# A graph network on one core: a squared tanh moved to ScalarE, a gate that reads PSUM, 23 of 50 row tiles weighed ahead, two gradient products moved up

## The chip, the cores and the metric

The kernel runs on one core of one Trainium2 chip. The metric is the device time of one execution in microseconds (us). TensorE (PE) multiplies matrices into PSUM, its accumulation memory of 8 banks of 512 fp32 columns; VectorE (DVE), ScalarE (ACT) and GpSimd (POOL) do the rest; SyncE (SP) only issues DMA transfers. Each engine runs its own instructions in the order in which they are written, and the engines meet only at semaphores (`wait_ge`, `then_inc`). An instruction that waits holds up all that stand behind it on its engine.

## The reference

x is 6250 nodes by 32 features; there are 106,250 directed edges (src, dst), sorted by dst. Four residual blocks follow one another: attention over the edges, five layers of graph convolution with normalisation, a gradient block, and a mean over the neighbours. The change touches the third, where the derivative of a scalar with respect to x is wanted:

```
def get_H(xx):
    z = xx @ W_fc.T
    e = sigmoid(concat([z[src], z[dst]]) @ W_attn.T)
    w = exp(e - emax[dst])
    h = segment_sum(w / denom[dst] * z[src], dst)
    h1 = segment_sum((h @ W_encK.T + b_encK)[src], dst)
    K = mlp3(h1, K_w0, K_b0, K_w1, K_b1, K_w2, K_b2)
    ue = (h @ W_p1.T + b_p1)[src] + (h @ W_p2.T + b_p2)[dst]
    U = mlp3(ue, ...)      # per edge: w2 @ relu(w1 @ tanh(w0 @ ue + b0) + b1) + b2
    return sum(segment_sum(K[src] * U, dst))
dHdx = grad(get_H)(x)      # then dHdx @ J.T - dHdx @ D.T
```

Its backward pass needs, for every edge, the tanh t of the first layer of U, its slope 1 - t*t, and the gate "relu of the second layer is above zero"; for every pair of nodes that has edges, the weight exp(sigmoid) and its derivative; and for every node three products that add up to the gradient of h.

## The kernel before

Edges lie as 128 partitions by 832 columns. Node data lies as 50 row tiles of 128 nodes (`NT` = 50). Sums over edges that can't be done by a scan over sorted edges are done as dense products with a table of counts, 6400 by 6400, that lies in DRAM.

The parts that matter here follow one another in this order:

- **The edge network ("the MLP loop"), 26 steps of 32 edge columns each.** A step's tanh values are `UT` (128 x 2048). They are taken in four pieces (`UG` = 4): PE transposes a piece (L2381) to `psT`, ACT copies it to SBUF (L2212), PE adds bias (L2395) and weight product (L2400) into one of **two** PSUM banks `psO`, ACT writes the relu to `UM` (L2214). DVE makes the slope as -t*t (L1963, 128 x 2048), the gate `hb` times the K row of the edge (L1967, four pieces), and PE and ACT take `hb` down through the transposed weights (L2381, L2235, L2417); DVE multiplies by the slope (L1977), copies (L1982) and runs a scan over sorted edges (L624, L629). Ahead of each step stands another scan (`spread_step`, L624 and L629) that repeats a node's row over its edges, and the sum that is fed to tanh (L1955). In DVE's order the gates of step k stand first, then `spread_step(k + 1)`, then the multiplication by the slope and the scan of step k. In ACT's order `up_act(k + 1)` (tanh, copies and relus) is followed by the store of step k, by `source_act(k + 2)` (L2197, which turns the loaded rows round into `UXP`), and that by `mask_act(k + 2)` (L2201, L2203), for which `spread_step(k + 2)` on DVE waits.
- **GpSimd beside it** gathers rows for the loop: 52 groups of 16 indirect DMAs (L485, `arena<-t_a`), and after these scatters the loop's results to `xd`: again 52 groups of 16 (L488), each with a load of its rows (L2525). After scatter group `HD_AT` = 29 it runs `ends_pool("umlp")`: one fetch to `joined`, a wait for DVE's `ends_dve`, a put, and 50 fetches of the loop's sums. After group `GK_AT` = 37 it fetches the rows that the K side needs.
- **Weighing ahead.** After the MLP loop, ACT and DVE make the weights of every third row tile (`BEFORE`, 17 of 50), for both halves of the columns and as two pieces each: 4 x 17 = 68 pieces of 128 x 1600 (tanh L1098, exp L1101, square L1103 on ACT; L1115 and L1120 on DVE). A piece's two results are stored to `weighed_cells` (1.6 MB). DVE does `ends_dve("umlp")` only behind all of them.
- **The K side and four quarters of a dense product** (L801, L747, L787, L869), while GpSimd goes on scattering.
- **The last scan ("dsum"),** 26 steps, once all is scattered, then `ends_pool("dsum")`.
- **The gradient of h,** `to_nodes_pe("dhf", ...)` (L787, L790): for each of 50 tiles three products (`DFM1` with `WD1`, `DFM2` with `WD2`, `SUMS3` with `fold`) into one place in PSUM. Only `DFM2` comes from the last scan.
- **The back stage:** two phases of 50 row tiles. A tile that was weighed ahead is read from DRAM (two pieces of 1.6 MB) into a ring of five buffers; the others are made by ACT (L1028, L1030, L1032) and DVE (L1042, L1048) as two pieces each. PE takes either (L1053).

The order is written out by hand on every engine; no planner chooses it.

Of the kernel before, what the change touches and what calls it, by code (L numbers as in the profile page):

```python
# [8 lines left out]
P = 128  # L9
# [69 lines left out]
def build(nc, x_in, src_in, dst_in, src_t_in, w_in, weights_in, vectors_in, out):  # L79
    ctx = ExitStack()  # L80
    with ctx:
# [146 lines left out]
        BEFORE = range(0, NT, 3)  # L228
# [143 lines left out]
        ALIAS_AT, XK_AT, GK_AT, HD_AT = 768, 15, 37, 29  # L372
# [421 lines left out]

        def to_features_pe(pe, name, source, banks):
# [295 lines left out]
        def ahead_act(act):  # L1091
            act.wait_ge(S["crossed"], TURN["umlp"] + 1)
            base = 4 * NS
            for i, j, phase, t, h in ahead():
                if j % len(BEFORE) == 0 and h == 0:
                    act.wait_ge(S[f"other{phase}"], 16 * 2)
                tanh = AHEAD_TANH[i % 2]
                act.activation(tanh, piece_of(AHEAD_OTHER[phase], h), ACT.Tanh, bias=a_dst[:, t:t + 1])  # L1098
                act.drain()
                act.wait_ge(S["weighed"], base + max(0, 2 * i - 1))  # L1100
                act.activation(AHEAD_EXP, tanh, ACT.Exp, scale=0.5, bias=half[:]).then_inc(S["weights_made"], 1)  # L1101
                act.wait_ge(S["weighed"], base + 2 * i)
                act.activation(AHEAD_SQUARE, tanh, ACT.Square).then_inc(S["weights_made"], 1)  # L1103
# [508 lines left out]
        def _(dve):  # L1612
# [346 lines left out]
            for k in range(2 * IT):  # L1959
                b = k % 2  # L1960
                slope, hb, dr = rows(UG2[b], 64), rows(UHB, 64), rows(UDR[b], 64)
                dve.wait_ge(S["umlp_tanh"], UG * (k + 1))
                dve.scalar_tensor_tensor(slope, rows(UT, 64), -1.0, rows(UT, 64), ALU.mult, ALU.mult)  # L1963
                for u in range(UG):
                    t = slice(8 * u, 8 * u + 8)
                    dve.wait_ge(S["umlp_relu"], UG * k + u + 1)
                    dve.scalar_tensor_tensor(hb[:, t, :], turned(UM[b], 64)[:, t, :], 0.0, turned(UXP[b], 64)[:, t, :], ALU.is_gt,  # L1967
                                             ALU.mult).then_inc(S["umlp_slope"], 1)
# [3 lines left out]
                for u in range(UG):  # L1972
# [4 lines left out]
                    last = dve.scalar_tensor_tensor(dr[:, t, :], slope[:, t, :], 1.0, DTURN[u % 2].rearrange("p (j f) -> p j f", f=64),  # L1977
# [82 lines left out]
            for made, t, got in node_banks("dhf", 32, bank):  # L2060
# [90 lines left out]
        def _(act):  # L2151
# [53 lines left out]
            def up_act(k):  # L2205
# [4 lines left out]
                for u in range(UG):  # L2210
# [4 lines left out]
                                   psO[u % 2].rearrange("p (j f) -> p j f", f=64), ACT.Relu).then_inc(S["umlp_relu"], 1)  # L2215

# [12 lines left out]
            for k in range(2 * IT):  # L2229
# [3 lines left out]
                for u in range(UG):  # L2233
                    act.wait_ge(S["umlp_turned"], 2 * UG * k + UG + u + 1)
                    act.copy(packB[u % 2], psT[u % 2]).then_inc(S["umlp_turned_copied"], 1)  # L2235
# [51 lines left out]
        def _(pe):  # L2287
# [96 lines left out]
            def up_pe(k):  # L2384
                n = 2 * UG * k
                for u in range(UG + 1):
# [350 lines left out]
```

## Time and profile before

| | us |
|---|---|
| median of 3 runs | 9476.88 (9472.27 to 9494.99) |
| the profiled execution | 9485.84 |
| its span | 9484.0 |

| engine | busy us | share |
|---|---|---|
| PE | 4877.8 | 51% |
| DVE | 4601.9 | 49% |
| ACT | 2819.5 | 30% |
| POOL | 5429.2 | 57% |

No engine is busy all the time, since the parts have different limits. One has to read each part by itself: where it starts and ends, which engine works without a gap in it, and for what the others wait. The profiled execution's own time is 1.8 us above its span.

### The profile page before, as it was taken

Reading aid. Unit: us, or ns where it says so; the run is one execution under the profiler, and the core shown is the slowest. Engines: PE = TensorE matmul, PEld = TensorE weight load, DVE = VectorE, ACT = ScalarE, POOL = GpSimd, SP = SyncE. Lnnn points to the kernel's source line nnn. Section 1 sums busy time; section 2 is a strip of 40 time slices with the busy share of each in tenths; the row PEclk is TensorE's granted clock in tenths of the full one; section 3 lists DMA queues with packets and bytes.
Section 4 is the critical chain, followed back from the end, with each engine's and each line's share of the span. In section 5 each row is a group of like instructions: output and inputs, shape, how many; then the busy total and the mean of one; then the engine's idle time right before and its main releaser. Section 6 shows DMA issues by size and latency. Waiting matters only on the chain.

```text
span 9484.0 us, 77287 instructions
## 1 busy us (share of the span) xinstructions
PE 4877.8 (51%) x27914; PEld 2625.5 (28%) x27914; DVE 4601.9 (49%) x6100; ACT 2819.5 (30%) x2192; POOL 5429.2 (57%) x5420
## 2 busy tenths in 40 slices
PE   1000007999257777775577665344440035038976
PEld 0000006888112232331222222244430023032333
DVE  5677776777000000000298960388885510428870
ACT  0111110000000000000198950266667600429850
POOL 3777767777777777777520017688877777320000
PEclk5555555555578989887698975676765568559986
DMA  8666536443398989999799999455559948538767
GB/s 186 215 222 220 205 83 137 154 153 141 155 415 356 415 359 411 365 362 415 279 283 268 288 204 379 144 202 206 203 191 370 342 147 336 187 85 282 263 222 291
DMA packets 1203136, 2404.24 MB, mean 254 GB/s; under 512 B 566439, under 2 KB 818794, under 8 KB 1171354
## 3 DMA queue, kind: packets, MB, share of 16 engines
q1 hardware_dynamic: 996986, 2076.35, 61.7%
q0 software_dynamic: 187136, 170.29, 6.9%
q10 hardware_dynamic: 18720, 153.79, 4.2%
q8 instruction: 171, 2.80, 0.1%
q14 instruction: 123, 1.01, 0.0%
HBM read 1606.44 MB, written 711.62 MB: 244 GB/s over the span
## 4 chain that ended last, share of the span: by engine, by line
POOL 37%; DMA 25%; issue 12%; PE 11%; ACT 7%; ACTq 4%; DVE 3%; SPq 1%; DVEq 0%; POOLq 0%
POOL arena L485 18%; DMA arena<-cells_w 14%; POOL xd L488 9%; POOL cells_w L488 9%; DMA arena<-cells_c 8%; PE ps L698 6%; ACT arena L1030 3%; ACTq L1029 3%; ACT arena L1028 2%; PE ps L787 2%; PE ps L879 1%; ACTq L2266 1%; PE ps L1053 1%; PE ps L1161 1%; DMA arena<-hot 1%
## 5 line engine op out<-in xcount | busy, mean ns | idle before, releaser
L698 PE MATMUL ps<-arena 128*64 128x458 f32 (+2 forms) x7252 | 1349.0, 655 | 701.2 <-DMA arena<-cells_w 699.7
L485 POOL DMA_INDIRECT arena<-t_a,arena x832 | 945.9, 1137 | 1094.9 <-DMA t_a<-arena 841.7
L1053 PE MATMUL ps<-arena 128*33 128x400 f32 x6336 | 1165.1, 522 | 310.1 <-DVE arena L1048 302.4
L488 POOL DMA_INDIRECT sorted<-arena x832 | 839.7, 1009 | 288.9 <-issue 288.9
L716 DVE COPY carry<-ps 64x128 f32<-64x128 f32 (+1 forms) x5 | 1.5, 295 | 2048.2 <-PE ps L698 2048.2
L488 POOL DMA_INDIRECT xd<-arena x832 | 832.7, 1001 | 256.4 <-issue 253.2
L488 POOL DMA_INDIRECT cells_c<-arena x832 | 810.5, 974 | 292.6 <-issue 292.6
L488 POOL DMA_INDIRECT cells_w<-arena x832 | 813.0, 977 | 276.8 <-issue 276.8
L485 POOL DMA_INDIRECT arena<-t_kv,idx x832 | 816.9, 982 | 258.7 <-issue 253.3
L698 PEld LDWEIGHTS ps<-arena 128*64 128x64 f32 (+1 forms) x7252 | 426.2, 147 | 1621.1 <-issue 856.4
L1053 PEld LDWEIGHTS ps<-arena 128*33 128x33 f32 x6336 | 366.6, 115 | 1106.4 <-issue 652.8
L1555 ACT ACTIVATE norm_cols<-norm_cols 128x1 f32<-128x1 f32 x5 | 1.0, 203 | 2235.0 <-DVE norm_cols L1537 2235.0
L1042 DVE TENSOR_TENSOR arena<-arena 128x1600 f32<-128x1600 f32 x328 | 597.3, 1821 | 96.0 <-ACT arena L1032 42.9
L1270 PE MATMUL ps<-arena 128*128 128x50 bf16 x832 | 72.4, 219 | 1055.3 <-DVE arena L1258 1055.3
L1048 DVE SCALAR_TENSOR_TENSOR arena<-arena 128x1600 f32<-128x1600 f32 x328 | 598.8, 1826 | 25.9
L629 DVE TENSOR_TENSOR_SCAN arena<-ps,arena 128x512 f32<-128x512 f32 (+2 forms) x494 | 591.4, 1263 | 7.6
L1030 ACT ACTIVATE arena<-arena,half 128x1600 f32<-128x1600 f32 x328 | 534.5, 1630 | 24.5 <-issue 2.4
L1369 PE MATMUL ps<-arena,packT 128*128 128x50 f32 x1664 | 434.8, 412 | 0.0
L1369 PEld LDWEIGHTS ps<-arena,packT 128*128 128x128 f32 x1664 | 434.7, 336 | 0.0
L879 PE MATMUL ps<-arena 128*64 128x400 f16 x1568 | 280.9, 508 | 248.3 <-DMA arena<-cells_c 227.6
L1032 ACT ACTIVATE arena<-arena 128x1600 f32<-128x1600 f32 x246 | 374.2, 1521 | 0.0
L801 PE MATMUL ps<-ident,arena 128*64 128x128 f32 x300 | 20.7, 308 | 652.4 <-DVEq L209 651.7
(536 smaller groups left out, 9097.3 us busy)
## 6 DMA issues: line engine op xcount, KB each, us to landing
arena<-cells_w SPq DMA_DIRECT2D x245, 3200.0 KB
arena<-cells_c SPq DMA_DIRECT2D x294, 800.0 KB, 5.3
arena<-cells_turned SPq DMA_DIRECT2D x200, 800.0 KB, 8.5
cells_w<-arena SPq DMA_DIRECT2D x49, 3200.0 KB, 20.4
weighed_cells<-arena SPq DMA_DIRECT2D x68, 1600.0 KB, 14.4
arena<-weighed_cells SPq DMA_DIRECT2D x68, 1600.0 KB, 7.2
cells_c<-arena SPq DMA_DIRECT2D x50, 1600.0 KB, 5.8
cells_turned<-arena SPq DMA_DIRECT2D x100, 800.0 KB, 5.4
```

Of the source, the lines that this page charges most:

```text
L485: return pool.indirect_dma_start(dst, None, table, bass.IndirectOffsetOnAxis(ap=index, axis=0))
L488: return pool.indirect_dma_start(table, bass.IndirectOffsetOnAxis(ap=index, axis=0), source, None)
L629: dve.tensor_tensor_scan(to[:, piece], mask[:, 0:n * CJ], buf[:, piece], 0.0, ALU.mult, ALU.add)
L698: mm = pe.matmul(bank[base + k][g * f:(g + 1) * f, 0:m], rows_of, tile[:, g * width + at:g * width + at + m], start=first, stop=last, skip ...
L879: mm = pe.matmul(bank[(4 if i == 0 else 0) + c][64 * g:64 * g + 64, 0:400], pieces, moving[:, a:a + 400], start=first, stop=last, skip_gro ...
L1029: act.drain()
L1030: last = act.activation(expo[b], tanh[b], ACT.Exp, scale=0.5, bias=half[:])
L1032: last = act.activation(tanh[b], tanh[b], ACT.Square)
L1042: last = dve.tensor_tensor(expo[b], expo[b], piece_of(counts_of(name, p), h), ALU.mult)
L1048: dve.scalar_tensor_tensor(tanh[b], tanh[b], -1.0, expo[b], ALU.add, ALU.mult).then_inc(S["weighed"], 1)
L1053: last = pe.matmul(bank[4 * h + c][64 * kind:64 * kind + 33, 0:400], own[:, t, :], moving[:, 400 * c:400 * c + 400], start=t == 0, stop=do ...
L1369: pe.matmul(to[:, 0:NT], packT[k % 2][:, i * P:(i + 1) * P], snap[k % 2][:, i * NT:(i + 1) * NT], start=True, stop=True, skip_group_check= ...
```

## The change

Four edits, in the places named above.

1. **MLP loop.** DVE's slope instruction (L1963) goes. ACT squares `UT` into `UG2` behind the four relus of a step. The sign is put into the copy of the transposed gates (scale -1) and into the constant of L1977. The gates `hb` read `psO`, the PSUM bank, where they read `UM`. So PE may write a bank of `psO` only once DVE has read it: a second wait stands before L2395.
2. **Weighing ahead.** 23 of 50 row tiles, spread evenly, where there were 17: 92 pieces and not 68. ACT's tanh of the next piece is issued between the exp and the square of this one.
3. **Places in GpSimd's row.** `HD_AT` 29 becomes 33, `GK_AT` 37 becomes 41.
4. **Gradient of h.** The products of `DFM1` and of `SUMS3` are made before PE's part of the last scan's end, into banks 4 to 7; only the product of `DFM2` is left behind it.

```diff
-        BEFORE = range(0, NT, 3)
+        BEFORE = [t for t in range(NT) if t * 23 % NT < 23]
...
-        ALIAS_AT, XK_AT, GK_AT, HD_AT = 768, 15, 37, 29
+        ALIAS_AT, XK_AT, GK_AT, HD_AT = 768, 15, 41, 33
...
+        def gradient_pe(pe, source, weight, first):
+
+            if not first:
+                pe.wait_ge(S["fm_taken"], STEP["dhf"])
+            for t in range(NT):
+                to = bank[4 + t // 16][:, t % 16 * 32:t % 16 * 32 + 32]
+                g, at = t // (NT // 2), t % (NT // 2) * P
+                a = slice(64 * g, 64 * g + 64)
...
+                last = pe.matmul(to, source[a, at:at + P], weight[a, :], start=first and t % 16 == 0, stop=not first,
+                                 skip_group_check=True)
+                if first:
+                    last = pe.matmul(to, SUMS3[0:96, t * P:t * P + P], fold[32][0:96, 0:32], start=False, stop=False,
+                                     skip_group_check=True)
...
             for k in range(2 * IT):
                 b = k % 2
                 slope, hb, dr = rows(UG2[b], 64), rows(UHB, 64), rows(UDR[b], 64)
-                dve.wait_ge(S["umlp_tanh"], UG * (k + 1))
-                dve.scalar_tensor_tensor(slope, rows(UT, 64), -1.0, rows(UT, 64), ALU.mult, ALU.mult)
                 for u in range(UG):
                     t = slice(8 * u, 8 * u + 8)
                     dve.wait_ge(S["umlp_relu"], UG * k + u + 1)
-                    dve.scalar_tensor_tensor(hb[:, t, :], turned(UM[b], 64)[:, t, :], 0.0, turned(UXP[b], 64)[:, t, :], ALU.is_gt,
-                                             ALU.mult).then_inc(S["umlp_slope"], 1)
+                    dve.scalar_tensor_tensor(hb[:, t, :], psO[u % 2].rearrange("p (j f) -> p j f", f=64), 0.0,
+                                             turned(UXP[b], 64)[:, t, :], ALU.is_gt, ALU.mult).then_inc(S["umlp_slope"], 1)
...
                                    psO[u % 2].rearrange("p (j f) -> p j f", f=64), ACT.Relu).then_inc(S["umlp_relu"], 1)
+                act.activation(UG2[k % 2], UT, ACT.Square)
...
                     if UG * k + v >= 2:
                         pe.wait_ge(S["umlp_relu"], UG * k + v - 1)
+                        pe.wait_ge(S["umlp_slope"], UG * k + v - 1)
...
+            await_made(pe, "dh_made")
+            gradient_pe(pe, DFM1, WD1, True)
             ends_pe(pe, "dsum", OD, 64, bank[3])
             await_made(pe, "dd_made")
             to_features_pe(pe, "DD", nodes(DD, 64), 4)
-            await_made(pe, "dh_made")
-            to_nodes_pe(pe, "dhf", DFM1, 64, 32, lambda c: WD1[64 * c:64 * c + 64, :], bank,
-                        more=((DFM2, 64, lambda c: WD2[64 * c:64 * c + 64, :]), (SUMS3, 96, lambda c: fold[32][0:96, 0:32])))
+            gradient_pe(pe, DFM2, WD2, False)
```

On PE, in the third and fourth product of a step's way up; before (L2381 is the transposition, L2395 the bias, L2400 the weight product):

```order
L2381 MATMUL ps<-ident,arena 128x128 [waits umlp_turned_copied,umlp_tanh]
L2381 MATMUL ps<-ident,arena 128x128 x3
L2395 MATMUL ps<-bias_parts,ones_bf 128x512 [waits umlp_relu]
L2400 MATMUL ps<-weights,packT 128x128 [waits umlp_turned_copied]
L2400 MATMUL ps<-weights,packT 128x128 x3
L2395 MATMUL ps<-bias_parts,ones_bf 128x512 [waits umlp_relu]
```

and now (L2407, L2422, L2427 are the same three):

```order
L2407 MATMUL ps<-ident,arena 128x128 [waits umlp_turned_copied,umlp_tanh]
L2407 MATMUL ps<-ident,arena 128x128 x3
L2422 MATMUL ps<-bias_parts,ones_bf 128x512 [waits umlp_slope,umlp_relu]
L2427 MATMUL ps<-weights,packT 128x128 [waits umlp_turned_copied]
L2427 MATMUL ps<-weights,packT 128x128 x3
L2422 MATMUL ps<-bias_parts,ones_bf 128x512 [waits umlp_slope,umlp_relu]
```

The order is the same; the bias product now waits for `umlp_slope`, which DVE's gates give. For the third product of step k it is the first gate of step k.

On ACT, the end of one step's way up and what stands behind it; before (L2214 relu, L2241 store, L2197 `source_act`, L2201 and L2203 `mask_act`):

```order
L2212 COPY packT<-ps 128x512
L2214 ACTIVATE arena<-ps 128x8x64
L2241 DMA d_edges<-arena 128x2048
L2197 COPY arena<-arena 128x4096
L2201 CAST ps<-same_s 128x16x31
L2203 CAST first_same<-same_s 128x1
```

and now, with what each waits for (L2241 is now the square, L2267 the store, L2222 `source_act`):

```order
L2237 COPY packT<-ps 128x512 [waits umlp_turned]
L2239 ACTIVATE arena<-ps 128x8x64 [waits umlp_up]
L2241 ACTIVATE arena<-arena 128x2048
L2267 DMA d_edges<-arena 128x2048 [waits umlp_taken]
L2222 COPY arena<-arena 128x4096 [waits umlp_slope,loaded1]
L2226 CAST ps<-same_s 128x16x31 [waits scanned]
L2228 CAST first_same<-same_s 128x1
```

One instruction is added, between the last relu and the store.

On PE, from the end of the quarters to the back stage, now (L889 quarters, L807 and L810 `gradient_pe`, L664 the end of the last scan, L821 the transposition of its sums; L807 below it is the product of `DFM2`):

```order
L889 MATMUL ps<-arena 96x400 x3
L807 MATMUL ps<-folded,arena 128x32 [waits made]
L810 MATMUL ps<-fold,arena 128x32
...
L664 MATMUL ps<-carry,equal_d 128x64 [waits carried]
L821 MATMUL ps<-ident,arena 64x128 [waits fm_taken,made]
...
L807 MATMUL ps<-folded,arena 128x32 [waits fm_taken]
L807 MATMUL ps<-folded,arena 128x32 x24
L807 MATMUL ps<-folded,arena 128x32 [waits group_done]
L807 MATMUL ps<-folded,arena 128x32 x24
```

100 of the 150 products stand ahead of L664 now; before, all stood behind it, three to a tile.

## Rows read from the trace of the kernel before

**Rows 1.** The page's part 4, the chain that ended last, by engine

```profile
POOL 37%; DMA 25%; issue 12%; PE 11%; ACT 7%; ACTq 4%; DVE 3%; SPq 1%; DVEq 0%; POOLq 0%
```

**Rows 2.** Timeline, one step: start us, us, engine, line, what, [idle before <-releaser]

```profile
6528.51 7.42 ACT L2197 COPY arena<-arena 128x4096 f32<-128x4096 f32 x1 [0.49 <-DMA arena<-a_edges]
6529.03 2.29 DVE L1963 SCALAR_TENSOR_TENSOR arena<-arena 128x2048 f32<-128x2048 f32 x1
...
6536.56 0.47 DVE L624 SCALAR_TENSOR_TENSOR arena<-spread_carry,first_same,arena 128x128 f32<-128x128 f32 x1 [0.85 <-ACT first_same L2203]
...
6555.64 0.38 PE L2395 MATMUL ps<-bias_parts,ones_bf 128*128 128x512 bf16 x1
...
6556.04 1.16 PE L2400 MATMUL ps<-weights,packT 128*128 128x128 f32 x8
...
6557.23 1.03 ACT L2214 ACTIVATE arena<-ps 128x512 f32<-128x512 f32 x1 [1.25 <-PE ps L2400]
...
6558.08 0.62 ACT L2212 COPY packT<-ps 128x512 f32<-128x512 f32 x1
```

**Rows 3.** Single lines: count, ns min/median/max, first and last start us

```profile
L1963 DVE SCALAR_TENSOR_TENSOR arena<-arena x26: 2291/2293/2297, 6092.4 to 7079.6; 128x2048 f32<-128x2048 f32 x26
...
L1967 DVE SCALAR_TENSOR_TENSOR arena<-arena x104: 1086/1177/1342, 6095.7 to 7085.0; 128x512 f32<-128x512 f32 x104
...
L1977 DVE SCALAR_TENSOR_TENSOR arena<-arena,ps x104: 664/687/715, 6118.7 to 7090.9; 128x512 f32<-128x512 f32 x104
...
L1032 ACT ACTIVATE arena<-arena x246: 1517/1521/1527, 4707.3 to 9139.8; 128x1600 f32<-128x1600 f32 x123
```

**Rows 4.** Timeline: from the MLP loop's end to the last piece weighed ahead

```profile
7119.33 0.80 PE L664 MATMUL ps<-carry,equal_s 128*128 128x128 f32 x2 [28.50 <-DVEq L649]
7127.37 1.63 ACT L1098 ACTIVATE arena<-arena,a_dst 128x1600 f32<-128x1600 f32 x1 [14.78 <-DMA arena<-row_a_src]
...
7552.20 1.82 DVE L1120 SCALAR_TENSOR_TENSOR arena<-ps,arena 128x1600 f32<-128x1600 f32 x1
```

**Rows 5.** Stage 7127 to 7553: span, busy of PE, PEld, DVE, ACT, POOL, PEclk, DMA, GB/s

```profile
7127.00:7553.00 426.00, 0.00 (x0) 0.00 (x0) 247.06 (x136) 315.02 (x204) 326.95 (x346) 0.50 1.05 373
```

**Rows 6.** DMA queues from 7140 to 7540: packets, MB, share of 16 engines

```profile
q1 hardware_dynamic: 82453, 129.51, 90.8%
q0 software_dynamic: 12458, 19.98, 14.2%
```

**Rows 7.** Timeline of GpSimd and DVE: two group loads, the join

```profile
7116.83 0.58 POOL L2525 DMA_DIRECT2D arena<-d_edges  x1
...
7137.81 0.58 POOL L2525 DMA_DIRECT2D arena<-d_edges  x1
...
7631.13 1.00 POOL L485 DMA_INDIRECT joined<-runs,join_s  x1 [0.30 <-issue]
...
7633.78 0.29 DVE L655 TENSOR_TENSOR joined<-joined,ps 128x128 f32<-128x128 f32 x1 [79.75 <-DMA joined<-runs,join_s]
```

**Rows 8.** Timeline of GpSimd: three gather instructions of one MLP step

```profile
6530.07 2.07 POOL L485 DMA_INDIRECT arena<-t_a,arena  x1 [0.30 <-issue]
...
6532.44 4.09 POOL L485 DMA_INDIRECT arena<-t_a,arena  x1 [0.30 <-issue]
...
6550.68 0.94 POOL L485 DMA_INDIRECT arena<-t_a,arena  x1 [0.30 <-issue]
```

**Rows 9.** Timeline of DVE: the start of the last scan

```profile
8175.72 1.03 DVE L2039 COPY arena<-arena 128x1024 f32<-128x1024 f32 x1 [113.69 <-DMA arena<-xd]
```

**Rows 10.** Timeline of PE: the three gradient products, two tiles

```profile
8449.16 0.63 PE L787 MATMUL ps<-folded,arena 64*128 64x32 f32 x2
...
8450.71 0.63 PE L787 MATMUL ps<-folded,arena 64*128 64x32 f32 x2
```

**Rows 11.** Timeline of PE in the back stage; a row is three tiles

```profile
8711.26 16.31 PE L1053 MATMUL ps<-arena 128*33 128x400 f32 x96 [0.83 <-DVE arena L1048]
8728.42 16.31 PE L1053 MATMUL ps<-arena 128*33 128x400 f32 x96 [0.84 <-DVE arena L1048]
```

More of the change, by code:

```diff
@@ L793, in to_nodes_pe @@
                     last.then_inc(S["fm_made"], 1)
+        def gradient_pe(pe, source, weight, first):
[5 more added lines that the diff above has]
+                a = slice(64 * g, 64 * g + 64)
+                if t == NT // 2:
+                    last.then_inc(S["group_done"], 1)
+                    groups_done[0] += 1
+                    pe.wait_ge(S["group_done"], groups_done[0])
+                last = pe.matmul(to, source[a, at:at + P], weight[a, :], start=first and t % 16 == 0, stop=not first,
[3 more added lines that the diff above has]
+                                     skip_group_check=True)
+                elif t % 16 == 15 or t == NT - 1:
+                    last.then_inc(S["fm_made"], 1)
         def to_features_pe(pe, name, source, banks):
@@ L1093, in ahead_act, with tanh_act @@
             base = 4 * NS
-            for i, j, phase, t, h in ahead():
+            todo = list(ahead())
+            def tanh_act(i):
+                _, j, phase, t, h = todo[i]
                 if j % len(BEFORE) == 0 and h == 0:
                     act.wait_ge(S[f"other{phase}"], 16 * 2)
-                tanh = AHEAD_TANH[i % 2]
-                act.activation(tanh, piece_of(AHEAD_OTHER[phase], h), ACT.Tanh, bias=a_dst[:, t:t + 1])
+                act.activation(AHEAD_TANH[i % 2], piece_of(AHEAD_OTHER[phase], h), ACT.Tanh, bias=a_dst[:, t:t + 1])
+            tanh_act(0)
+            for i in range(len(todo)):
                 act.drain()
                 act.wait_ge(S["weighed"], base + max(0, 2 * i - 1))
-                act.activation(AHEAD_EXP, tanh, ACT.Exp, scale=0.5, bias=half[:]).then_inc(S["weights_made"], 1)
+                act.activation(AHEAD_EXP, AHEAD_TANH[i % 2], ACT.Exp, scale=0.5, bias=half[:]).then_inc(S["weights_made"], 1)
+                if i + 1 < len(todo):
+                    tanh_act(i + 1)
                 act.wait_ge(S["weighed"], base + 2 * i)
-                act.activation(AHEAD_SQUARE, tanh, ACT.Square).then_inc(S["weights_made"], 1)
+                act.activation(AHEAD_SQUARE, AHEAD_TANH[i % 2], ACT.Square).then_inc(S["weights_made"], 1)
         def ahead_dve(dve):
@@ L1976, in _ @@
                         dve.wait_ge(S[f"d_kept{b}"], CREDIT + 16 * (k // 2))
-                    last = dve.scalar_tensor_tensor(dr[:, t, :], slope[:, t, :], 1.0, DTURN[u % 2].rearrange("p (j f) -> p j f", f=64),
+                    last = dve.scalar_tensor_tensor(dr[:, t, :], slope[:, t, :], -1.0, DTURN[u % 2].rearrange("p (j f) -> p j f", f=64),
                                                     ALU.add, ALU.mult)
@@ L2059, in _ @@
             dhf = nodes(DHF, 32)
-            for made, t, got in node_banks("dhf", 32, bank):
+            for made, t, got in node_banks("dhf", 32, bank[4:8]):
                 dve.wait_ge(S["fm_made"], made)
@@ L2234, in _ @@
                     act.wait_ge(S["umlp_turned"], 2 * UG * k + UG + u + 1)
-                    act.copy(packB[u % 2], psT[u % 2]).then_inc(S["umlp_turned_copied"], 1)
+                    act.activation(packB[u % 2], psT[u % 2], ACT.Copy, scale=-1.0).then_inc(S["umlp_turned_copied"], 1)
                 if k >= 1:
```

## The prediction

> **What bounds the kernel now.** I read the chain of waits first: by engine, 37% of it is GpSimd, 25% DMA and 11% PE [rows 1]. Followed in order of time, it runs on GpSimd from the middle of the MLP loop until all results are scattered, then over the last scan, then over PE in the back stage. So an edit counts only as far as it moves GpSimd's row of gathers and scatters, the last scan, or PE behind it.
>
> Then the timeline of one step of the MLP loop [rows 2]. DVE starts the slope at 6529.03 and the next `spread_step` at 6536.56, 7.53 us later, having waited 0.85 us for ACT's mask. ACT began to turn the next rows round (L2197) at 6528.51, before DVE's gates. That is what makes the loop fit: ACT's relus of a step are done while DVE is still in its scan. A step takes (7079.6 - 6092.4) / 25 = 39.5 us by the starts of L1963 [rows 3].
>
> Then the hand-over. The loop ends at about 7120, weighing ahead runs from 7127.4 to 7554.0 [rows 4], and DVE has then idled 79.75 us when GpSimd comes to the join at 7631.1 [rows 7]. So the join waits for GpSimd now, and DVE is 80 us early. A scatter group takes 7137.81 - 7116.83 = 20.98 us [rows 7]. The last scan starts at 8175.7, where DVE has waited 113.69 us for scattered rows [rows 9]: the K side and the quarters are hidden with that much to spare. In the back stage PE works 16.31 us of every 17.16 [rows 11].
>
> **The MLP loop.** The new wait says: the third product of step k may start only once DVE has done the first gate of step k. On DVE this gate stands behind the whole scan of step k - 1. On ACT, the relus of pieces 3 and 4 stand ahead of the square, the next source copy and the next mask, and for this mask DVE waits with its next `spread_step`. So what ran beside the scan is now a chain behind it, once a step:
> - first gate: between 0.69 (L1977, one operand in PSUM) and 1.18 (L1967, both in SBUF) [rows 3]; I take 0.93;
> - bias and product 0.38 + 1.16, relu 1.03, copy 0.62, product 1.16, relu 1.03 [rows 2]: 5.4, and with some 0.05 for each of six hand-overs 5.7;
> - the square of 128 x 2048: at least the 1.52 of 1600 columns (L1032), at most the 2.29 that DVE needs for the same size [rows 3]; by columns 1.52 x 2048 / 1600 = 1.95; I take 1.9;
> - from the start of the source copy to the start of `spread_step`, 6536.56 - 6528.51 = 8.05 [rows 2].
>
> Together 16.6 us from DVE's first gate to its next `spread_step`, against 7.53: 9.1 a step. The removed 2.29 of DVE and the shorter gates are inside this and buy nothing, as DVE waits for ACT. I take 9.0 (8 to 10). For 25 steps this is 225 us, and about 3 for the last, in which the square stands ahead of the first copy downward: the loop ends 228 us later, and the first piece is weighed at 7355 and not at 7127.
>
> **Weighing ahead.** A piece takes (7554.0 - 7127.4) / 68 = 6.27 us [rows 4]. ACT is busy for 315.02 / 68 = 4.63 of it, and the DMA engines are full, at a share of 1.05 and 373 GB/s [rows 5]; so the reordered tanh buys nothing here. 14.2 points of the share are GpSimd's own scatters [rows 6]. Once GpSimd stands still, a piece can take 6.27 x 90.8 / 105 = 5.4; I take 5.5 (4.63 to 6.27).
>
> When does GpSimd stand still? It comes to the join 4 groups later, 4 x 20.98 = 84, but earlier by what DVE no longer costs it: beside L1963 and L1967 its gathers take 2.07 and 4.09 us where 0.94 is the rule, and beside L1977 0.94 [rows 8, 2], so 1.13 + 3.15 = 4.3 a step and up to 111 in 26. That makes 7631 + 84 - 111 = 7604 (up to 7715). From 7355 to 7604 there are 249 / 6.27 = 39.6 pieces, and the other 52.4 take 288: 7892, and with the last stores in flight (a piece and a half) 7900. GpSimd waits there some 300 us, and all 18 scatter groups left are queued behind that wait, as are the fetches for the K side.
>
> The join is thus at 7900 where it was at 7634 [rows 7]: +266. Behind it stand 18 groups and not 22: -84. The last scan starts 182 us later, at about 8358. The K side and the quarters move by 266 as well, since `GK_AT` keeps its distance of 8 groups from `HD_AT`; of the 113.69 us to spare [rows 9] some 30 are left, so they cost nothing.
>
> **The gradient products.** A tile's three products take 8450.71 - 8449.16 = 1.55 us [rows 10], so one takes 0.52 (at most its 0.63 of busy time). Behind the last scan 50 tiles now take 26 us and not 78: -51 (-46 to -52). The other 100 products, 52 us, lie between 8175.7 and 8449 of before [rows 9, 10], where PE has nothing but the ends of the scan to do.
>
> **The back stage.** A row of 96 is six pieces: 2.72 us of PE each, 272 for the 100 of a phase, and a wait of 0.84 in every three tiles, 14 us a phase [rows 11]. With 54 made pieces and not 66, ACT and DVE are ahead, and up to 28 us in both phases could go. But a phase now reads 46 x 1.64 + 27 x 0.82 = 97.5 MB, 261 us at the 373 GB/s of [rows 5], beside PE's 272: nearly two bounds at once. I take half, -14 (-28 to +5).
>
> **Sum.** +182 - 51 - 14 = +117 on the profiled execution's 9485.8: 9603. The median of the runs is 9 lower: 9594. The bounds: 8 to 10 us a step is 25 either way in the loop and, since fewer pieces then lie beside GpSimd's scatters, 22 in the sum; a piece at 4.63 or 6.27 is -46 or +40; GpSimd at 7715 is +14; then +5 and -14 to +19. The forecast's own range is 9520 to 9670.
>
> **Rivals.**
> - *The loop keeps its pace.* The gate in PSUM costs nothing, and the freed DVE and GpSimd time comes through. For it: PE and ACT both have gaps in a step (1.25 us before each relu [rows 2]). Against it: the gate is behind the scan in DVE's own order, and no gap of PE can change that. Then weighing ahead starts at 7127, 76 pieces are done by 7604, the other 16 by 7692, the join is at 7700: +66 - 84 - 51 - 14 = -83, median 9394. It decides if a step stays under about 42 us. If GpSimd's stalls also stay as they are, it comes at 7715, the join moves by 84, and -65 is left: 9412.
> - Where that rests on GpSimd: the rows show gathers of 4.09 us beside an instruction with two inputs in SBUF and 0.94 beside one with a PSUM input [rows 8]. The Trainium skill (SBUF — State Buffer, "Who interferes with whom") says that a VectorE instruction with at most one SBUF input does not contend with GpSimd, and the trace agrees. It also says that one with two contends only with GpSimd instructions that read SBUF, and infers that making DMA descriptors needs the write side alone; by that there would be nothing to free, and the rival's time would be 9412. The 4.09 speaks against that part.
> - *The loop loses half of it,* 4.5 us a step, as ACT finds the third product sooner than I think, or a later load sets the pace either way. Then 113 us of the delay go, 101 in the sum: +16, median 9493, no change that can be told. Against it: the terms of the chain are all from rows, and only the square and the first gate are estimates, 1.3 us between them.
> - *The back stage turns DMA-bound.* At 330 GB/s its 97.5 MB take 295 us a phase where a phase takes 286 now (50 / 3 x 17.16): +9 a phase and not -7, median 9626, inside the forecast's range.
>
> **How the numbers follow.** The forecast, with the DMA-bound back stage in it, has 0.80; the loop at its old pace 0.13; half 0.07. Under 0.3%, 28 us, this kernel's change can't be told from none: so faster means under 9448, and that is the first rival alone, 0.13; no change is most of the third, 0.06; slower is the rest, 0.81. The range of 9480 to 9680 takes in nearly all of the forecast and part of the third; the first rival stays out.
>
> **What would show it.** In the profile after: starts of the gates 48.5 us apart, where L1963 had 39.5; DVE idle for some 9 us before L624 of `spread_step`, released by ACT's mask; PE's bias product released by DVE; the loop's end near 7348. Weighing ahead near 5.5 us a piece once GpSimd is still. GpSimd idle for about 300 us before its put of `joined`, released by DVE. Gathers of 4 us gone. The last scan starting near 8358, DVE idle there about 30 us. 26 us from the first `DFM2` product to the last. PE in the back stage with gaps under 0.8 us in three tiles, released by DMA if at all. The forecast is wrong if the gates come 40 us apart, if GpSimd doesn't wait at the join, or if weighing ahead is not held by DMA.

## The result, and the profile after

| | before | after |
|---|---|---|
| median | 9483.46 us (4 runs, 9472.27 to 9494.99) | 9565.3 us (4 runs, 9558.28 to 9572.54) |
| profiled execution | 9485.84 | 9572.54 |
| its span | 9484.0 | 9570.7 |

The changed kernel takes 1.0086 times as long [1.0074, 1.0098]. Predicted was 9594, with a range of 9480 to 9680.

The chain of waits of the kernel after, by engine, to be read against [rows 1]: GpSimd has lost 14 points of the span; DVE, DMA and PE have gained 8, 5 and 5. Up to the join the end is now reached over the MLP loop (DVE's scans, PE, ACT) and weighing ahead, not over GpSimd's gathers and scatters; behind the join it still runs over GpSimd's scatters.

```profile
DMA 30%; POOL 23%; PE 16%; DVE 11%; issue 9%; ACT 7%; ACTq 3%; DVEq 1%; SPq 1%; POOLq 0%
```

The timeline of one step of the MLP loop after, all engines, in order of start. The last column is the idle time before it and what ended it. It answers to [rows 2, 8].

```profile
6522.12 1.06 POOL L485 DMA_INDIRECT arena<-t_a,arena  x1 [0.30 <-issue]
6522.45 1.94 DVE L1992 SCALAR_TENSOR_TENSOR arena<-ps,arena 128x512 f32<-128x512 f32 x2
6523.49 0.95 POOL L485 DMA_INDIRECT arena<-t_a,arena  x1 [0.30 <-issue]
6523.60 0.59 PE L2422 MATMUL ps<-bias_parts,ones_bf 128*128 128x512 bf16 x1 [8.53 <-DVE arena L1992]
...
6525.93 1.03 ACT L2239 ACTIVATE arena<-ps 128x512 f32<-128x512 f32 x1 [9.80 <-PE ps L2427]
...
6529.49 1.90 ACT L2241 ACTIVATE arena<-arena 128x2048 f32<-128x2048 f32 x1
...
6531.28 7.11 ACT L2222 COPY arena<-arena 128x4096 f32<-128x4096 f32 x1
...
6539.02 0.53 DVE L624 SCALAR_TENSOR_TENSOR arena<-spread_carry,first_same,arena 128x128 f32<-128x128 f32 x1 [8.27 <-ACT first_same L2228]
```

Read it as a chain. DVE's first gate (L1992) starts at 6522.45. PE has waited 8.53 us for it with the bias of the third piece (L2422); ACT has waited 9.80 us for PE. Two relus with a copy of a transposed piece between them, the square (1.90) and the source copy (7.11) follow, and only then the mask, for which DVE has waited 8.27 us (0.85 before). From first gate to next `spread_step` it is 6539.02 - 6522.45 = 16.57 us; the prediction's sum was 16.6.

The gates as one line, (count, ns min/median/max, first and last start), and then `spread_step`'s first instruction from the groups by line of 6080 to 7320 us (count, busy us, mean ns, idle before):

```profile
L1992 DVE SCALAR_TENSOR_TENSOR arena<-ps,arena x104: 1002/1030/1054, 6095.9 to 7294.3; 128x512 f32<-128x512 f32 x104
```

```profile
L624 DVE SCALAR_TENSOR_TENSOR arena<-spread_carry,first_same,arena 128x128 f32<-128x128 f32 x25 | 11.8, 474 | 199.7 <-ACT first_same L2228 199.7
```

DVE's wait for the mask is 199.7 / 25 = 8.0 us a step. The gates of one step and the next start 6570.33 - 6522.45 = 47.9 us apart. Over all 25 intervals the mean is (7287.03 - 6095.88) / 25 = 47.65: 8.2 above the 39.5 of [rows 3].

Then the hand-over: ACT's last copy of the loop (released by DVE's last carry, L631, at 7313.96), its first piece weighed ahead, GpSimd's fetch for the join, DVE's last piece, the join, GpSimd's put behind it, and DVE at the start of the last scan. They answer to [rows 4, 7, 9].

```profile
7314.32 7.14 ACT L2247 COPY arena<-arena 128x4096 f32<-128x4096 f32 x1 [7.05 <-DVE carry L631]
...
7337.11 1.63 ACT L1120 ACTIVATE arena<-arena,a_dst 128x1600 f32<-128x1600 f32 x1 [15.66 <-DMA arena<-row_a_src]
...
7604.64 1.00 POOL L485 DMA_INDIRECT joined<-runs,join_s  x1 [0.30 <-issue]
...
7869.04 1.82 DVE L1147 SCALAR_TENSOR_TENSOR arena<-ps,arena 128x1600 f32<-128x1600 f32 x1
7880.98 0.29 DVE L655 TENSOR_TENSOR joined<-joined,ps 128x128 f32<-128x128 f32 x1 [10.12 <-DMA weighed_cells<-arena]
...
7881.57 0.98 POOL L488 DMA_INDIRECT runs<-joined,join_s x1 [275.93 <-DVEq L656]
...
8338.77 1.04 DVE L2064 COPY arena<-arena 128x1024 f32<-128x1024 f32 x1 [30.45 <-DMA arena<-xd]
```

The idle time has changed sides. Before, DVE stood 79.75 us at the join and GpSimd arrived last; now GpSimd stands 275.93 us, and DVE arrives last. The stretch of weighing ahead, cut where GpSimd stops (span, then busy of PE, PEld, DVE, ACT, POOL, then PEclk, DMA share, GB/s; [rows 5]):

```profile
7337.00:7604.00 267.00, 0.00 (x0) 0.00 (x0) 154.15 (x85) 196.77 (x130) 205.07 (x217) 0.50 1.05 374
7604.00:7875.00 271.00, 0.00 (x0) 0.00 (x0) 181.30 (x100) 220.93 (x146) 1.34 (x2) 0.50 1.06 379
```

The DMA share is full in both. What GpSimd's scatters leave goes to ACT and DVE, whose busy shares rise by 11% and 16%.

PE at the gradient and at the start of the back stage; a row is one group of products ([rows 10]):

```profile
8597.72 7.76 PE L821 MATMUL ps<-ident,arena 128*64 128x128 f32 x100 [69.98 <-DVEq L209]
8606.26 19.46 PE L807 MATMUL ps<-folded,arena 64*128 64x32 f32 x100 [0.78 <-DVE arena L2083]
8631.95 7.64 PE L1073 MATMUL ps<-arena 128*33 128x400 f32 x32 [6.23 <-DVEq L209]
```

And inside the back stage, PE after ([rows 11]), with a window of 240 us that starts 74 us behind the stage's first product, after and then before:

```profile
8739.81 67.38 PE L1073 MATMUL ps<-arena 128*33 128x400 f32 x400 [1.50 <-DVE arena L1068]
...
8811.32 70.06 PE L1073 MATMUL ps<-arena 128*33 128x400 f32 x416 [0.77 <-DVE arena L1068]
```

```profile
8706.00:8946.00 240.00, 233.35 (x1388) 82.62 (x1384) 186.81 (x113) 199.49 (x129) 0.00 (x0) 0.99 0.99 353
```

```profile
8600.00:8840.00 240.00, 226.39 (x1334) 77.04 (x1332) 223.77 (x126) 235.36 (x154) 0.00 (x0) 1.00 0.82 288
```

PE's rows are longer (400 products without a wait, where 96 were) and the gaps fewer: in the whole stage PE waits for DVE 12 times and 36.1 us, where it was 31 times and 52.2, and one wait near the start is 24.5 us of either. So, that one apart, 11.6 us are left to gain there by more tiles, and DMA's share has gone from 0.82 to 0.99.

The 86.7 us between the two spans, by stretch:

| stretch | before | after | difference |
|---|---|---|---|
| start of the last scan | 8175.7 | 8338.8 | +163.1 |
| the last scan | 259.0 | 258.9 | -0.1 |
| its end to the back stage's first product | 90.8 | 34.2 | -56.6 |
| two phases of the back stage | 690.8 | 668.4 | -22.4 |
| what follows | 267.7 | 270.4 | +2.7 |

### The profile page after: what moved, and what is told of

The parts are those of the page before. It is cut to its first block, busy times and chain, and to the rows that moved or that the text cites. A ratio compares the mean times of both kernels' runs of the same rounds, so it can differ in the third digit from the quotient of the medians.

```text
span 9570.7 us, 77448 instructions
## 1 busy us (share of the span) xinstructions
PE 4858.6 (51%) x27914; PEld 2632.1 (28%) x27914; DVE 4529.2 (47%) x6068; ACT 2859.7 (30%) x2224; POOL 5329.3 (56%) x5420
## 4 chain that ended last, share of the span: by engine, by line
DMA 30%; POOL 23%; PE 16%; DVE 11%; issue 9%; ACT 7%; ACTq 3%; DVEq 1%; SPq 1%; POOLq 0%
DMA arena<-cells_w 14%; POOL arena L485 10%; POOL cells_w L488 9%; DMA arena<-cells_c 8%; PE ps L698 5%; DVE arena L629 4%; PE ps L1073 4%; DMA weighed_cells<-arena 4%; POOL xd L488 3%; ACT arena L2222 2%; ACT arena L1050 2%; ACTq L1049 1%; PE ps L787 1%; ACT arena L1048 1%; PE ps L2444 1%
## 5 line engine op out<-in xcount | busy, mean ns | idle before, releaser
L485 POOL DMA_INDIRECT arena<-t_a,arena x832 | 832.4, 1001 | 1095.3 <-DMA t_a<-arena 842.0
L1062 DVE TENSOR_TENSOR arena<-arena 128x1600 f32<-128x1600 f32 x304 | 553.5, 1821 | 172.4 <-DMA arena<-cells_turned 127.1
L1068 DVE SCALAR_TENSOR_TENSOR arena<-arena 128x1600 f32<-128x1600 f32 x304 | 555.0, 1826 | 24.3 <-issue 0.4
L1050 ACT ACTIVATE arena<-arena,half 128x1600 f32<-128x1600 f32 x304 | 495.4, 1629 | 21.8 <-issue 1.0
L2444 PE MATMUL ps<-weights,arena 128*128 128x128 f32 x832 | 192.5, 416 | 471.9 <-ACT arena L2261 247.1
L821 PE MATMUL ps<-ident,arena 128*64 128x128 f32 x300 | 21.2, 312 | 689.4 <-DVEq L209 688.7
```

Of the source, the lines that this page charges most:

```text
L485: return pool.indirect_dma_start(dst, None, table, bass.IndirectOffsetOnAxis(ap=index, axis=0))
L1050: last = act.activation(expo[b], tanh[b], ACT.Exp, scale=0.5, bias=half[:])
L1062: last = dve.tensor_tensor(expo[b], expo[b], piece_of(counts_of(name, p), h), ALU.mult)
L1068: dve.scalar_tensor_tensor(tanh[b], tanh[b], -1.0, expo[b], ALU.add, ALU.mult).then_inc(S["weighed"], 1)
L2444: last = pe.matmul(DTURN[v % 2][:, i * P:(i + 1) * P], packB[v % 2][:, i * P:(i + 1) * P], weights[:, down:down + P], start=True, stop=True)
```

## The experiments

Theory: PE's wait for the first gate makes the step 8 us longer; everything ahead of the last scan follows from it; ScalarE's square, the 23 tiles and the gradient save a little each. Rivals: the square itself, or the read of PSUM, costs the time; or the six extra tiles do. ACT's reordered tanh in weighing ahead stays in all runs but b.

**Undo the loop's edit alone (a_noloop).** The first of each pair is the kernel after; ACT's copies downward and the constant of the multiplication by the slope get their old signs as well:

```
-  dve.scalar_tensor_tensor(hb[:, t, :], psO[u % 2]..., 0.0, turned(UXP[b], 64)[:, t, :], ALU.is_gt, ALU.mult)
+  dve.wait_ge(S["umlp_tanh"], UG * (k + 1))
+  dve.scalar_tensor_tensor(slope, rows(UT, 64), -1.0, rows(UT, 64), ALU.mult, ALU.mult)
+  dve.scalar_tensor_tensor(hb[:, t, :], turned(UM[b], 64)..., 0.0, turned(UXP[b], 64)[:, t, :], ALU.is_gt, ALU.mult)
-  act.activation(UG2[k % 2], UT, ACT.Square)
-  pe.wait_ge(S["umlp_slope"], UG * k + v - 1)
```

> The changed kernel with the MLP loop as it was before (slope on DVE, gates from UM, no second wait on PE, copies with scale 1); 23 tiles, HD_AT 33, GK_AT 41 and the split gradient stay. The theory (the gate's wait makes the loop longer, and GpSimd then stands at the join): the loop ends at 7120 again, 92 pieces at 6.27 us end at 7704, and with the last stores 12 us later DVE is at the join at 7716, where GpSimd comes at 7631 + 84 = 7715. Join +84, 18 groups behind it and not 22: -84. Gradient -57 and back stage -22 as measured in the changed kernel: span 9408, ratio to before 0.992. The rival that weighing 24 more pieces is what costs: still slower than before, ratio above 1.003.

Measured: 9421.51 us, ratio 0.9931 [0.9915, 0.9948]. The slope starts 39.7 us apart, the join is at 7716.73, and DVE idles 32.33 us ahead of the last scan. So all the other edits together make the kernel faster, and the loop's edit alone turns this round.

**The loop's edit alone on the kernel before (b_looponly).** The same lines the other way.

> The kernel before with the MLP loop of the changed one, nothing else. The theory: a step takes 47.7 us as in the changed kernel, the loop ends some 210 us later, at 7329; GpSimd comes to the join at 7520 and stands there until 68 pieces are done: 29 beside its scatters, 39 at 5.3 us, 7739 with the last stores. So +105 us: ratio 1.011. The rival that the loop is hidden behind GpSimd (it was early at the join before): ratio within 0.3% of 1.

Measured: 9590.01, ratio 1.0105 [1.0088, 1.0122]. The join is at 7741.0, and DVE's idle time before the last scan stays at 112.7: nothing else has taken the delay up. GpSimd is at the join 110 us earlier (7521.3, before 7631.1) and waits there for it. The loop's edit costs 101 us here (1.05%) and 144 in the kernel after (9565.3 - 9421.5); f, below, shows where most of the difference lies.

```profile
7741.63 0.97 POOL L488 DMA_INDIRECT runs<-joined,join_s x1 [219.34 <-DVEq L656]
```

**The loop's edit in two halves (c_squareonly, d_gateonly).** The first is the kernel after with gates from `UM` and without PE's wait; the second keeps these two and lets DVE make the slope.

> The changed kernel, but the gates read UM in SBUF as before and PE doesn't wait for them; ACT still squares. The theory that the wait is the cause: the square lies behind relus that are done beside the scan, and the source copy starts 1.3 us later than the load alone would let it; a step takes 40.0 to 40.8 us, the loop ends 15 to 35 us later than before, the span is 9410 to 9440, ratio 0.992 to 0.996. The rival that ScalarE is the bound and its square the cause: a step near 47 us, ratio near 1.009.

> The changed kernel, but DVE makes the slope as before (L1963, 2.2 us ahead of the gates) and ACT doesn't square; the gates read PSUM and PE waits for them. The theory: the chain loses the square's 1.9 us and gains the slope's 2.2 ahead of it: a step takes 48 us, ratio 1.008 to 1.012. The rival that the square is the cause: a step near 39.5 us and a ratio near 0.992.

Measured: c 9417.3, ratio 0.9928 [0.9911, 0.9945]; d 9599.79, ratio 1.0114 [1.0097, 1.0131]. The slope of d has its starts 48.65 us apart, those of a 39.7; the gates of c about 39.9:

```profile
L1990 DVE SCALAR_TENSOR_TENSOR arena<-arena x26: 2291/2292/2294, 6095.8 to 7312.1; 128x2048 f32<-128x2048 f32 x26
```

So the square isn't it. It does push the mask back (DVE waits 4.0 us a step for it in c), but DVE has 2.29 us less to do. Nor is the square a gain: c differs from a in it alone, and 9417.3 can't be told from 9421.51. (Two bounds of what was expected of c were missed, both to the good side: a step of 39.9 where 40.0 was the least, and the loop's end 10 us later than before, 7113.67, where 15 was.) The gate's half is the whole loss. That half is two edits in one, which the next run parts.

**PE's wait without the read of PSUM (j_waitonly).** The kernel after, with gates that read `UM`, and PE's wait for them kept:

```
-  dve.scalar_tensor_tensor(hb[:, t, :], psO[u % 2]..., 0.0, ...
+  dve.scalar_tensor_tensor(hb[:, t, :], turned(UM[b], 64)[:, t, :], 0.0, ...
```

> The changed kernel with the gates read from SBUF (the relus that ScalarE stored) and the matrix engine's wait for them kept. Theory (the wait costs the 8 us a step, and not the read of PSUM): the gates start 47.5 to 48.5 us apart, the mask comes 8 us late again, and VectorE reaches the join 150 us or more behind the kernel without the wait (7722 us): 7870 to 7910; GpSimd's gathers beside the gates are stretched again, so its fetch to the join comes near 7685 and not at 7605; ratio 1.009 (1.007 to 1.012). Rival (the read of PSUM, or VectorE and ScalarE at one bank, makes the step longer): the gates 39.5 to 42 us apart, ratio under 1.000.

Measured: 9592.75, ratio 1.0106 [1.0088, 1.0124].

```profile
L1992 DVE SCALAR_TENSOR_TENSOR arena<-arena x104: 1094/1156/1216, 6096.4 to 7310.2; 128x512 f32<-128x512 f32 x104
```

```profile
6528.34 0.59 PE L2422 MATMUL ps<-bias_parts,ones_bf 128*128 128x512 bf16 x1 [8.33 <-DVE arena L1992]
```

PE waits 8.33 us for the gate, DVE 8.12 for the mask, and the join is at 7903.6, inside the 7870 to 7910 expected. The wait makes the step longer, whatever the gate reads: j differs from c in PE's wait alone, and the first gates start 48.3 us apart, where they do 39.9 in c. One number missed: GpSimd came to the join at 7639 and not near 7685. That is taken up in the last section.

**GpSimd not held (e_hd46).** `GK_AT, HD_AT = 41, 33` become `48, 46`, so that the join comes when weighing ahead is done.

> The changed kernel with both positions of the last joined group moved behind the work made ahead, so that neither GpSimd nor VectorE stands at the join. Theory (the time is set by how long the weighing ahead takes, with its transfers at the queues' rate, and GpSimd's standing for 276 us is only the other side of it): with all 92 pieces beside the scatters, VectorE reaches the join near 7337 + 92 x 6.2 + 12 = 7919 us; GpSimd's gathers, 428 us behind their fetch, are then covered or nearly so; the last scan starts at 8290 to 8340 (8339 in the changed kernel), span 9520 to 9570, ratio 1.003 to 1.009. Rival (GpSimd's 276 us on its own are the loss): the last scan starts 100 us earlier or more, span under 9470, ratio below 0.999.

Measured: 9530.33, ratio 1.0052 [1.0036, 1.0069]. The join is at 7917.4, 36 us later than in the kernel after, and yet the last scan starts at 8292.9, 46 us earlier. The rival's 100 us did not come. Only 46 of the 276 us in which GpSimd stood come back. By its row alone the last scan would start 13 groups of 20.98 us earlier behind the later join, 8338.8 + 36 - 273 = 8102, and its last scatter is indeed issued at 8126.8. What ends last now is the K side, which starts at the join: GpSimd waits 33.47 us for the table before it fetches the K side's rows at 8065.1 (8122.7 in the kernel after), and DVE then waits for PE's quarters. DVE's waits from 8080 to 8360 (total us, times, longest):

```profile
DVE arena L958 <- PE ps L889: 205.2, 4, 51.7
DVE arena L2064 <- DMA arena<-xd: 7.5, 1, 7.5
```

**17 tiles and not 23 (f_weigh17).** `BEFORE = range(0, NT, 3)` again, with positions 37 and 29; the rest is the kernel after.

> The changed kernel with 17 row tiles weighed ahead in place of 23 and the last joined group's positions as before; the loop's edit and the two gradient products stay. Theory: the extra tiles do not pay for themselves at this loop: the join comes at 7738 us (as with the loop's edit alone), the last scan starts near 8278 after an idle of some 113 us, the gradient saves 57, the back stage has the 22 us back that the six tiles took from it; span 9530 (9515 to 9545), ratio 1.005 (1.003 to 1.007). Rival (the extra tiles hide the loop's loss in part): without them the span is above 9571, ratio over 1.009.

Measured: 9531.11, ratio 1.005 [1.0033, 1.0067], span 9529.3 where 9530 was expected; join 7739.7, last scan at 8281.95 behind 114.3 us of idle time. With the longer step the six extra tiles and their positions cost 34 us (9565.3 - 9531.1). With the step as it was, a_noloop with them is 9421.51 and g_gradonly, next, without them 9424.62: no difference that can be told. So the extra tiles bring nothing at these positions, and cost where the loop is longer.

**The gradient's change alone (g_gradonly).** The kernel before with two of a tile's three products made ahead; all three add up in four banks of their own. (ACT's reordered tanh is in as well; the last scan starts 3 us later than before, so it buys nothing here.) `+` is this run, `-` the kernel before, cut to the calls:

```
+  gradient_pe(pe, DFM1, WD1, True)       # ahead of the last scan's end: DFM1 x WD1, SUMS3 x fold
-  to_nodes_pe(pe, "dhf", DFM1, 64, 32, ..., more=((DFM2, 64, ...), (SUMS3, 96, ...)))
+  gradient_pe(pe, DFM2, WD2, False)
```

> The kernel before with only the gradient's change: two of the three products made in the last scan's shade. Theory: nothing ahead of the last scan's end moves; the stretch from its end to the back stage's start goes from 90.8 to 34.2 us; span 9427 (9420 to 9435), ratio 0.994 (0.993 to 0.995). Rival (TensorE's products inside the scan hold it up, and part of it is given back): the last scan longer than 259 us by 10 or more, ratio above 0.996.

Measured: 9424.62, ratio 0.9938 [0.9921, 0.9955]. The last scan starts at 8178.93. PE:

```profile
8437.78 7.74 PE L821 MATMUL ps<-ident,arena 128*64 128x128 f32 x100 [69.88 <-DVEq L209]
8446.30 19.48 PE L807 MATMUL ps<-folded,arena 64*128 64x32 f32 x100 [0.78 <-DVE arena L2085]
8472.00 7.62 PE L1073 MATMUL ps<-arena 128*33 128x400 f32 x32 [6.23 <-DVEq L209]
```

From the scan's end to 8472.0 it is as in the kernel after, and the scan isn't held up by the products laid beside it (8437.78 - 8178.93 = 258.9 us, 259.0 before). This edit is nearly all that the kernel after has gained apart from the loop: 9424.62 here, 9421.51 in a.

**A better kernel (i_best).** If the wait is what costs and the square is only badly placed, ScalarE should square where it has a gap. The timeline of ACT in the kernel after shows one ahead of its third copy downward:

```profile
6542.57 0.60 ACT L2261 ACTIVATE arena<-ps 128x512 f32<-128x512 f32 x1 [2.59 <-PE ps L2407]
```

So here is the kernel after, with c's gates, and:

```
-  act.activation(UG2[k % 2], UT, ACT.Square)      # behind the relus, ahead of the source copy
+  if u == 2:                                      # between the second and the third copy downward
+      act.activation(UG2[k % 2], UT, ACT.Square)
+  dve.wait_ge(S["umlp_turned_copied"], 2 * UG * (k - 1) + UG + 3)   # ahead of spread_step's sum, for k >= 1
+  dve.wait_ge(S["umlp_turned_copied"], 2 * UG * k + UG + 3)         # ahead of the multiplication by the slope
-  ALIAS_AT, XK_AT, GK_AT, HD_AT = 768, 15, 41, 33
+  ALIAS_AT, XK_AT, GK_AT, HD_AT = 768, 15, 42, 34
```

> The changed kernel with the gates read from SBUF again, without the matrix engine's wait for them; ScalarE squares the tanh, but behind its second downward copy and not ahead of the source copy; VectorE's first pass waits for the last copy behind it; the last joined group one position later (34 and 42). Theory: the loop's step keeps 39.7 us or less (the kernel before's), the join comes near 7717, the last scan starts at 8160 to 8170 with VectorE idle 10 to 30 us ahead of it; span 9380 to 9400, ratio 0.990 to 0.992. Rival (any square on ScalarE in the step costs its own length, 1.9 us x 26): step 41.6, span 9440 or more, ratio 0.995 or more.

Measured: 9391.02, ratio 0.9898 [0.9882, 0.9915]: faster than both kernels, and than c (0.9928; the intervals touch, but each of the four runs is below each of c's). The step, by the gates' starts:

```profile
L1994 DVE SCALAR_TENSOR_TENSOR arena<-arena x104: 1100/1175/1335, 6097.3 to 7082.1; 128x512 f32<-128x512 f32 x104
```

```profile
6537.98 0.46 DVE L624 SCALAR_TENSOR_TENSOR arena<-spread_carry,first_same,arena 128x128 f32<-128x128 f32 x1 [1.76 <-ACT first_same L2231]
6538.52 7.91 DVE L629 TENSOR_TENSOR_SCAN arena<-ps,arena 128x512 f32<-128x512 f32 x7
6538.80 1.93 ACT L2263 ACTIVATE arena<-arena 128x2048 f32<-128x2048 f32 x1
```

The last gate is at 7082.1, where before it was at 7085.0 [rows 3]: the square's 1.93 us lie wholly beside DVE's scan. Join 7721.6, DVE idle 11.5 us ahead of the last scan, which starts at 8162.3: all sides come to it at nearly one time.

Of the 26 us to c, the square's place is not shown to have won any. The last piece is weighed 11.6 us earlier than in c (7701.0, there 7712.6), but DVE then waits 20.59 us at the join for GpSimd, and the join is where it was in c, 7721.6 and 7722.0. What starts the last scan 17.6 us earlier (8162.3, there 8179.9) is by these rows the one group fewer (20.98 us) behind the join, from the positions 34 and 42. By c's trace it had room for that too: GpSimd came to the join at 7687.1, 35 us ahead of DVE, and DVE idled 30.5 us ahead of the last scan. c at these positions was not run.

## Why the prediction was right

The place and the sign were right, and the runs show them: by a and b the loop's edit is the loss, by c, d and j it is PE's wait for the first gate. By its own steps:

- **The MLP step.** 9.0 longer was forecast and 8.2 measured. The chain of 16.57 us in the step above equals its sum, but in part because terms cancel: 7.04 us to the start of the square (6.63 taken), 1.79 from there to the source copy (1.9), 7.74 from there to `spread_step` (8.05). Gates took 1.03 us (0.93 taken). The first part is longer because PE comes out of its 8.53 us of waiting at a granted clock of 0.50 (the column ahead of the last two; 0.50 is 1.2 GHz) and takes 2.30 us for bias and product, where the prediction's rows, taken at 1.00, have 1.56 from start to end. After, then before:

```profile
6523.60:6525.90 2.30, 2.30 (x10) 1.94 (x10) 0.78 (x1) 0.00 (x0) 1.78 (x2) 0.50 0.16 29
```

```profile
6555.60:6557.20 1.60, 1.58 (x13) 1.19 (x12) 1.46 (x2) 0.39 (x1) 1.52 (x1) 1.00 1.01 211
```

  What made the forecast 0.8 too high is the other side of the difference. The 7.53 us from DVE's slope to its next `spread_step` were read from one step, and a fast one. Over the 25 steps before, this stretch has a mean of 8.2 us, since DVE's wait for the mask is 32.7 / 25 = 1.31 and not 0.85:

```profile
L624 DVE SCALAR_TENSOR_TENSOR arena<-spread_carry,first_same,arena 128x128 f32<-128x128 f32 x25 | 11.6, 466 | 32.7 <-ACT first_same L2203 32.4
```

  After, the stretch from the first gate to `spread_step` has a mean of 16.4, so 8.2 more. The rest of a step did not change: 31.3 us before, 31.2 after. The loop ends 210 us later (7313.96, before 7103.57), not 228.
- **Weighing ahead.** 6.27 us a piece beside the scatters held: 42 pieces from 7337 to 7604 are 6.36. Behind them, 50 in (7867.1 - 7602.8) = 5.29 us each; 5.5 was taken, and the bound worked out from the queues' shares was 5.4.
- **GpSimd at the join.** 7604 forecast, 7604.64 measured. The size of GpSimd's saving was right and its account was not, as the last section shows: in part this is luck. It waited 275.93, not 300.
- **The join** moved by 247 and not 266: 18 less from the loop's end. The 84 us of four groups held: 247.2 - 84 = 163.2, and the scan moved by 163.1. DVE's 30.45 us of idle time ahead of the scan are the 30 forecast, so the K side was covered, with nothing to spare beyond that.
- **The gradient.** -56.6, where -51 was taken and -52 was the bound. The 50 products left, two instructions each, take 19.46 us: 0.39 a product, not 0.52. PE's granted clock explains a part. These windows show two stretches of L807 after, then one of before:

```profile
8606.30:8612.00 5.70, 5.70 (x38) 5.70 (x39) 0.69 (x1) 0.00 (x0) 0.00 (x0) 0.72 0.00 0
...
8618.00:8625.70 7.70, 7.70 (x37) 7.58 (x36) 1.39 (x2) 0.00 (x0) 0.00 (x0) 0.50 0.00 0
```

```profile
8449.00:8475.00 26.00, 26.00 (x102) 23.82 (x101) 0.69 (x1) 0.00 (x0) 0.00 (x0) 0.50 0.00 1
```

  At the same 0.50 an instruction takes 7.70 / 37 = 0.208 us and took 26.00 / 102 = 0.255; at 0.72, a mean of both levels just behind L821, it takes 5.70 / 38 = 0.150. The mistake was to price one product of a mixed group of three as a third of it; for 100 instructions that is 25.5 - 20.8 = 4.7 us, and the higher clock at the start gave another 1.3 (20.8 - 19.46).
- **The back stage.** -22.4 where -14 (-28 to +5) was taken. The DMA-bound rival did not come about: the queues moved 353 GB/s at a share of 0.99, more than the 330 it needed to be slower. But its limit is near: DVE's wait for the other pieces' loads (L1062, `cells_turned`) grew from 24.9 us in the stage to 127.1, without holding PE up by as much (PE's waits for DVE fell from 52.2 us to 36.1).
- **The sum.** +117 forecast, +86.7 measured: the join is 19 of the difference, the gradient 6, the back stage 8, and the 2.7 at the end go the other way. But for that last one the errors had one sign.
- **The rivals.** The loop that keeps its pace was priced at 9394 to 9412; c, which is that case with the wait truly gone, ran in 9417.3. The loop that loses half, 4.5 us a step, is out by the 8.2 measured.

## What to carry to other kernels

When a consumer is moved from a copy in SBUF to the producer's own PSUM bank, the bank isn't free until that consumer is done (here 8.2 us a step): look at what stands ahead of it in its engine's order, and at what stands behind the next producer, before counting the time saved on the instruction. Work that is moved to another engine belongs in a gap of that engine, here 1.9 us of squares beside a scan, not ahead of what a third engine waits for. In i_best this ended the loop 12.7 us earlier than in c, time that then lay idle at the join. Don't take a stretch's length from one step when its steps differ: before, the same stretch took from 6.8 to 12.6 us. And when a stretch gets longer, set the positions of joins and the amount of work laid ahead again, as these had been set for the old lengths (the kernel after gains 35 us by two numbers alone).

## What was not expected of the hardware

- GpSimd's indirect DMAs are stretched by DVE's instructions in a way that depends on when they come. Beside DVE's four gates in one row, both inputs in SBUF, one gather takes 4.09 us [rows 8]. In j_waitonly the same gates stand apart, and GpSimd's timeline there is:

```profile
6527.05 2.16 DVE L1992 SCALAR_TENSOR_TENSOR arena<-arena 128x512 f32<-128x512 f32 x2
6528.10 1.94 POOL L485 DMA_INDIRECT arena<-t_a,arena  x1 [0.30 <-issue]
...
6531.59 0.95 POOL L485 DMA_INDIRECT arena<-t_a,arena  x1 [0.30 <-issue]
6531.73 1.15 DVE L1992 SCALAR_TENSOR_TENSOR arena<-arena 128x512 f32<-128x512 f32 x1 [2.51 <-ACT arena L2239]
...
6773.13 1.13 DVE L1992 SCALAR_TENSOR_TENSOR arena<-arena 128x512 f32<-128x512 f32 x1 [2.49 <-ACT arena L2239]
6773.25 1.84 POOL L485 DMA_INDIRECT arena<-t_a,arena  x1 [0.30 <-issue]
```

  The two stretched gathers started while a gate ran, and ended 0.83 us after it or its neighbour did (6529.21 and 6530.04, 6774.26 and 6775.09); the one that started 0.14 us ahead of a gate isn't stretched. So a row of gates can hold a gather for the rest of its length (not always: one that started at 6769.22 beside two gates took 1.24), and a single gate for its own at most. GpSimd's fetch at the join is at 7704.7 with the loop as before (a), 7687.1 without DVE's slope (c), 7639.2 with the gates apart as well (j), and 7604.64 when they also read PSUM: 17.6, 47.9 and 34.6 us (21.0, 47.6 and 39.4 when counted from GpSimd's first gather). The shares depend on the order: d, which is the kernel after with the slope on DVE, has the fetch at 7642.3, and there the slope costs 37.6. The prediction had put 1.13 x 26 = 29 us on the slope and the other 82 on the gates' operand, and none on their standing apart.
- The Trainium skill (SBUF — State Buffer, "Who interferes with whom") says that a VectorE instruction with two SBUF inputs contends with a GpSimd instruction that reads SBUF, not with one that only writes it; that the making of DMA descriptors needs the write interface is inferred there. The prediction took the 4.09 us to speak against this. They need not: these DMAs are indirect, and take the numbers of their rows from SBUF (`arena` is an input of each). GpSimd's plain DMAs have none, and the same gates don't hold them; in the kernel before:

```profile
6568.16 2.95 POOL L485 DMA_INDIRECT arena<-t_a,arena  x1 [0.30 <-issue]
6570.21 4.65 DVE L1967 SCALAR_TENSOR_TENSOR arena<-arena 128x512 f32<-128x512 f32 x4
6571.10 0.59 POOL L2497 DMA_DIRECT2D a_edges<-arena  x1
6571.99 3.72 POOL L485 DMA_INDIRECT arena<-t_a,arena  x1 [0.30 <-issue]
```

  The plain DMA takes 0.59 us in the middle of the gates (0.58 is its median), the gather behind it 3.72. So the section's rule fits if an indirect DMA is counted among what reads SBUF; that it is this read which is held was not tested by a run. What the operand is worth is shown: 34.6 us between j and the kernel after, which differ in one input of the gate alone. With one input in PSUM a gather takes 0.95; the same section has no contention for at most one SBUF input, outside the modes that use two ports.
- A copy with one SBUF input, of 128 x 2048, stretches a gather too, after as before (2.20 us there). The same section says that a copy can enter a mode that uses two ports and then blocks GpSimd for the whole instruction, and these rows agree:

```profile
6558.20 1.97 DVE L2007 COPY arena<-arena 128x2048 f32<-128x2048 f32 x1
6558.66 2.21 POOL L485 DMA_INDIRECT arena<-t_a,arena  x1 [0.30 <-issue]
```
